# Cross keys computed at the exit of a convolution, gate transposes moved behind two expert units, and a sigmoid table requested early

## What is computed

```python
x = x + L0_attn(layernorm(x))     # causal self-attention, 16 heads
x = x + L0_conv(layernorm(x))     # long convolution with a gate: y = irfft(rfft(kv)*rfft(k)) + kv*skip; out = y . ctx
x = x + L0_ffn(layernorm(x))      # mixture of experts: 2 shared, 16 routed
x = x + L1_attn(layernorm(x))     # causal self-attention
x = x + L1_xattn(layernorm(x), ctx)   # cross attention; its keys and values come from ctx alone
x = x + L1_ffn(layernorm(x))      # 32 experts, 4 per token

# L0_ffn
out = flat + sum_shared(relu(flat @ w1 + b1) @ w2 + b2)
scores = sigmoid(flat @ centroids.T) + bias
vals, idx = top_k(scores, 4)
gating = scatter(vals, idx); gating = gating / sum(gating)
out = out + sum_e gating[:, e] * (relu(flat @ w1[e] + b1[e]) @ w2[e] + b2[e])
```

## Time and profile before

| | us |
|---|---|
| median of three runs | 576.19 (575.97 to 577.64) |
| the profiled execution's own time | 570.98 |
| its span | 569.2 |
| from the end of the convolution's last product to the end of the router scores | 141.2 to 160.5 |
| from there to the first `down` | 160.5 to 168.9 |
| the expert loop on PE | 168.9 to 286.9 |

### The profile page before, as it was taken

How to read it: one execution, slowest core, us unless ns; L and a number is a source line. 1 busy time by engine, 2 the same in 40 slices (tenths; PEclk the granted TensorE clock), 3 DMA queues, 4 the chain that set the end, 5 groups by cost and what they waited for, 6 DMA issues and landing times.

```text
span 569.2 us, 13098 instructions
## 1 busy us (share of the span) xinstructions
PE 535.0 (94%) x4933; PEld 341.4 (60%) x4933; DVE 360.8 (63%) x795; ACT 259.6 (46%) x533; POOL 319.5 (56%) x395
## 2 busy tenths in 40 slices
PE   7999998999999999999998999987999998899998
PEld 4556765444656666665665566664555554466687
DVE  5456864999865555543487567776687757972341
ACT  2315553000395666563454355645566567104530
POOL 3448754989675444331044699859799973540000
PEclk9999999999999999999999999999999999999999
DMA  8996028000006333331303994011120022028311
GB/s 279 109 133 282 3 102 372 0 0 1 0 7 223 111 95 108 96 108 55 99 27 47 124 196 167 1 30 29 43 91 2 2 70 99 1 86 303 122 45 59
DMA packets 25134, 53.05 MB, mean 93 GB/s; under 512 B 3515, under 2 KB 16333, under 8 KB 23153
## 3 DMA queue, kind: packets, MB, share of 16 engines
q1 hardware_dynamic: 24357, 51.01, 32.7%
q10 hardware_dynamic: 716, 1.21, 0.6%
HBM read 41.51 MB, written 1.12 MB: 75 GB/s over the span
## 4 chain that ended last, share of the span: by engine, by line
PE 62%; DVE 17%; POOL 8%; ACT 5%; issue 4%; SPq 2%; DMA 1%; ACTq 0%; POOLq 0%; DVEq 0%
PE PS L1394 57%; POOL R L614 6%; PE PS L1398 4%; DVE R L1240 4%; DVE R L1237 3%; DVE mx L1141 2%; DVE R L424 2%; DVE xn L1029 1%; SPq L445 1%; PE PS L1417 1%; ACT xnT L754 1%; POOL rstd L563 1%; PE PS L1853 1%; DVE X L1019 1%; DVE stats L1014 1%
## 5 line engine op out<-in xcount | busy, mean ns | idle before, releaser
L1394 PE MATMUL PS<-R 128*128 128x256 f16 (+5 forms) x1864 | 184.6, 273 | 2.7 <-DVE R L1296 1.4
L1394 PEld LDWEIGHTS PS<-R 128*128 128x128 f16 (+4 forms) x1864 | 123.1, 102 | 70.6 <-issue 42.2
L1141 DVE TENSOR_REDUCE mx<-PS 128x4 bf16<-128x512 f32 x128 | 82.4, 686 | 36.5 <-PE PS L1394 27.3
L840 ACT ACTIVATE R<-PS 128x512 f32<-128x512 f32 x128 | 69.4, 594 | 65.3 <-PE PS L1394 65.1
L1394 PE MATMUL PS<-xnT,R 128*128 128x512 f16 (+1 forms) x348 | 83.3, 379 | 1.4 <-ACT xnT L754 1.4
L614 POOL TENSOR_TENSOR R<-mx,causal 128x512 bf16<-128x512 bf16 x64 | 65.5, 1044 | 31.7 <-DVE mx L1141 30.3
L1287 DVE TENSOR_TENSOR R<-R,wr 128x512 f32<-128x512 f32 (+1 forms) x46 | 33.3, 723 | 57.3 <-ACT R L939 53.6
L614 POOL TENSOR_TENSOR R<-mx,R 128x512 bf16<-128x512 bf16 x64 | 65.3, 1043 | 6.3 <-DVE mx L1141 6.2
L939 ACT ACTIVATE R<-PS,small 128x512 f32<-128x512 f32 (+1 forms) x50 | 34.3, 686 | 48.9 <-PE PS L1394 48.9
L1394 PEld LDWEIGHTS PS<-xnT,R 128*128 128x128 f16 (+1 forms) x348 | 33.8, 99 | 33.6 <-ACT xnT L754 2.0
L1394 PE MATMUL PS<-negidb,R 128*128 128x128 bf16 x512 | 41.9, 219 | 3.8 <-ACT R L840 2.0
(11 more groups left out here) (206 smaller groups left out, 819.2 us busy)
## 6 DMA issues: line engine op xcount, KB each, us to landing
R<-in_experts_dram SPq DMA_DIRECT2D x5, 1536.0 KB, 8.3
R<-R SPq DMA_DIRECT2D x48, 128.0 KB, 7.0
wr<-g_scr SPq DMA_DIRECT2D x16, 256.0 KB, 3.2
R<-in_w_dram SPq DMA_DIRECT2D x1, 3200.0 KB, 17.5
R<-in_w_dram SPq DMA_DIRECT2D x1, 3168.0 KB, 10.3
WT<-in_wt_a_dram SPq DMA_DIRECT2D x2, 1024.0 KB, 11.7
R<-in_toe_dram SPq DMA_DIRECT2D x1, 2048.0 KB, 13.9
wr<-g_scr SPq DMA_DIRECT2D x10, 192.0 KB, 2.8
```

The source lines that it names most:

```text
L840: s.activation(PTm[:, n % 4, 4 * k:4 * k + 4, :], bank(2 + (2 * n + k) % 3).rearrange("p (h q) -> p h q", h=4), ACT.Exp, scale=c["sc"]).th ...
L1141: v.tensor_reduce(mx[:, n % 4, 4 * k:4 * k + 4], bank(k).rearrange("p (h k) -> p h k", h=4), AX.X, ALU.max).then_inc(S("att_mx"), 1)
L1394: return nc.tensor.matmul(o_, l, r, start=start, stop=stop)
```

## The change

Three edits, all in the order of instructions; no arithmetic is added or removed, apart from fillers and one one-element activation.

1. **Cross keys earlier.** `cross_keys` takes the half as argument and uses banks 1 and 2. On PE the first half takes the place of the ten fillers behind the last skip product, and the second half the place of the ten fillers ahead of the turned sequences. ACT makes the bias of the first half behind `block_high(0..1)`, with waits for the last use of the context in `CT`, and of the second half behind the fourth copy of turned sequences. DVE makes the low part of the first half after the eighth `conv_update`, and of the second half, with the values' bias (`cross_rows`), after the last `normalise`. Fillers beside them use other banks, and `up(1)` and the router scores wait until the banks of the keys have been read.
2. **Gate transposes later.** They stand behind `down(0)`, `up(4)` and `down(1)`, in banks 2 and 3; PE waits for the copied gates only ahead of `down(4)`. ACT's `gates()` moves from unit 3 to unit 4.
3. **Sigmoid table early.** ACT runs a sigmoid on one element (`warm`) behind the first half of the keys.

```diff
@@ ACT
+            act.wait_ge(S("ub"), B)
+            act.wait_ge(S("wb_ready"), B)
+            cross_keys(0)
+            s.activation(warm[:, :], ident[:, 0:1], ACT.Sigmoid)
             for half in range(NH):
 ...
                 if half == 0:
+                    cross_keys(1)
                     weights_high("w16r", cen16[:, 0], cenT)
 ...
             for i in range(N0):
-                if i == 2:
-                    cross_keys()
-                if i == 3:
+                if i == 4:
                     gates()
@@ DVE
             for b in range(6, B):
                 conv_update(b)
+            cross_keys(0)
             for b in range(4, B):
                 normalise(2, b)
+            cross_keys(1)
+            cross_rows()
 ...
-                if i == 2:
-                    cross_keys()
@@ PE
-            def cross_keys():
-                pe.wait_ge(S("x_updated"), 2 * B)
-                for half in range(NH):
-                    for dc in range(DC):
-                        ins = mm(bank(6 + half, parts=64), wkv[:, 0, dc, :], ctxT[:, dc, half * HF:(half + 1) * HF], dc == 0, dc == 1)
-                    ins.then_inc(S("kx_ps"), 1)
+            def cross_keys(half):
+
+                pe.wait_ge(S("z"), DC * CH - 2 + half)
+                for dc in range(DC):
+                    ins = mm(bank(1 + half, parts=64), wkv[:, 0, dc, :], ctxT[:, dc, half * HF:(half + 1) * HF], dc == 0, dc == 1)
+                ins.then_inc(S("kx_ps"), 1)
 ...
-            keep_busy(10, 7)
+            cross_keys(0)
             pe.wait_ge(S("oT"), DC * CH)
 ...
-            keep_busy(10, 2)
+            cross_keys(1)
             for b in range(4):
                 xnt(2, b)
-                keep_busy(2, 2)
-            keep_busy(4, 2)
+                keep_busy(2, 0)
+            keep_busy(4, 0)
             pe.wait_ge(S("xnT_ready"), 2 * B + 4)
             up(0)
+            pe.wait_ge(S("kx_lo"), 1)
             up(1)
 ...
+            pe.wait_ge(S("kx_lo"), NH)
             pe.wait_ge(S("xnT_ready"), 3 * B)
 ...
-            cross_keys()
             up(2)
             up(3)
-            pe.wait_ge(S("gf0"), 1)
-            for b in range(B):
-                ins = tr(PS[0:NE0, 4 + b // 4, b % 4 * P:(b % 4 + 1) * P], gf0[:, b, :])
-                if b % 4 == 3:
-                    ins.then_inc(S("g0T_ps"), 1)
-            pe.wait_ge(S("g0T"), NH)
+
+            def gates_by_expert():
+                pe.wait_ge(S("gf0"), 1)
+                for b in range(B):
+                    ins = tr(PS[0:NE0, 2 + b // 4, b % 4 * P:(b % 4 + 1) * P], gf0[:, b, :])
+                    if b % 4 == 3:
+                        ins.then_inc(S("g0T_ps"), 1)
+
 ...
             for i in range(N0):
                 if 1 <= i < N0 - 3:
                     up(i + 3)
-                if i == 2:
-                    pe.wait_ge(S("kx_lo"), NH)
+                if i == 4:
+                    pe.wait_ge(S("g0T"), NH)
                 down(i)
+                if i == 1:
+                    gates_by_expert()
```

28 lines of the change are left out of this document (14 added, 14 removed).

## The result

Beside each other on one chip, in 20 runs each, the changed kernel has a median of 579.47 us (577.18 to 584.99) and the kernel before 576.02 (573.06 to 582.18). The ratio is 1.0068, with a 95% interval of 1.0044 to 1.0093. The time lies 1.1 above the forecast of 578.4 and inside the range.

The account below looks back on a forecast made before the run. PE, busy 94% of the span, was taken as the bound, without slack behind the first `down`. `down(3)` at 178.9 instead of 176.71 gave +2.2: 576.19 + 2.2 = 578.4 us, range 576.6 to 581.2.

Parts of the forecast that it names:

- The rival of the clock: PE's new idle stretches lower its clock to 1.2 GHz; one slow pair gives +4.8 us, 581.0; chance 0.12.
- list of signs: Wrong if PE has no gap ahead of down(3), first down is after 168, or clock below full at 161 to 190.
- Exit of the convolution: Four key instructions replace ten fillers, so the transposes start 0.3 us later, with ends 0.2 and 0.4.
- The second half of the keys: Ahead of the turned sequences: the first comes 0.24 us late, the next catch up; counted as nothing, at worst 0.2.
- Sigmoid: Without the table load beside the scores, the sigmoid follows them at about 160.8, 0.15 us earlier than before.
- Start of the experts: down(0) no longer waits behind gate transposes and ACT's copies; it starts at 167.27, 1.6 us earlier.
- `up(2)` and `up(3)` ... end well ahead; their time isn't on the path: Ahead of down(0), these products needn't wait for the keys and so add nothing to the time.
- The way round of the gates: From transposes through DRAM to first gated product: 6.4 us, upper end 7.04; that product starts at 177.6, 4.0 later.
- The order on DVE: Unit 3's low part stands behind unit 4's gated product, ends 1.3 us after its start, and delays down(3).
- The sum: down(3) starts at 178.9 instead of 176.71, +2.2 us, with ends +0.9 and +2.85.
- The slack ahead of `down(7)`: Of 2.5 us slack behind the fifth gated product 1.8 is used, 0.7 left; it holds, narrowly.
- The gaps forecast: PE idles 2.7 us behind the scores, 1.0 between up(3) and down(0), and 2.8 ahead of down(3).

Follow-up runs that it names:

- e3_fillers: The changed kernel with 24 filler matmuls between the scores and up(2); 582.49 us, ratio 1.0113 to the kernel before.
- e6_turn_first_fill: The changed kernel with gate transposes ahead of down(0), their wait still ahead of down(4), and 24 fillers ahead of up(2); 573.27 us, ratio 0.9950 to before.
- e10_turn_behind_first: The changed kernel with 24 fillers ahead of up(2) and gate transposes behind down(0) instead of down(1); 576.46 us, ratio 1.0005 to before.
- e9_both_filled: The changed kernel with 24 fillers ahead of up(2) and 26 ahead of down(3); 579.05 us, ratio 1.0071 to the kernel before.

## Why the prediction was right

The sign, the mechanism and the place were right: the gates come about as late as forecast, DVE meets them ahead of the low part of unit 3, and `down(3)` waits. The rival of the clock came true beside the forecast, not in its stead. By the prediction's own list of signs, two of the three that would show it wrong stand in the profile after: the first `down` at 28.25, which is 168.9 in the frame of before and later than 168, and a granted clock of 0.50 between 168 and 175 us. The third, a PE without a gap ahead of `down(3)`, doesn't. Point by point:

- **Exit of the convolution.** Mis-sized. +0.3 was forecast, with 0.4 as the upper end, and +0.50 measured (2.39 against 1.89). The transposes started 1.86 after the keys' start, so they waited for nearly all of the four passes (1.93); hardly any tail was saved. By the scores it had grown to +0.59. The second half of the keys, counted at nothing with 0.2 at worst, is left with the remaining 0.1: the first turned sequence came 0.87 late (10.96 against 10.09), and most of that was caught up as forecast.
- **Sigmoid.** It came 0.11 later, not 0.15 earlier, all of it from the term above: the scores are 0.59 late, and without a load the sigmoid follows them at once (0.87 idle, released by PE). The table alone gives the 0.47 that the step had in mind. The trace with the keys alone shows once more an activation that starts as its table load ends (163.00 + 1.28, then 164.29), as the earlier trace rows did, and no drain behind it, against the Trainium skill's figure (page "ScalarE: Activation LUTs", section "What ACT_TABLE_LOAD costs").
- **Start of the experts.** At full clock `down(0)` starts at 26.94, where the forecast had 26.6: the 0.3 of the two points above. In the profiled execution of the changed kernel it starts at 28.25, not earlier than before at all. The step "`up(2)` and `up(3)` ... end well ahead; their time isn't on the path" failed: at 1.2 GHz they end at 28.5 and are the path.
- **The way round of the gates.** 6.4 was forecast and 7.04 the upper end; it measured 6.4 with the gates alone, 6.55 with both gaps filled and 6.7 in the changed kernel, but 7.1 with the low part of unit 3 first and 8.6 with half of the keys early, so 7.04 is no bound for other orders. ACT did stand waiting (3.26) and copied as the transposes went.
- **The order on DVE.** As forecast: `down(3)` behind the first gated product by 1.35 (1.3 forecast), and taking the low part out of that place removes the wait.
- **The sum.** +2.2 forecast; 2.43 with the gates alone, 2.70 with all edits at full clock. The difference of 0.5 is 0.3 of the exit of the convolution, 0.15 of the way round and the rounding of the low part.
- **The slack ahead of `down(7)`.** "It holds, narrowly" failed in the profiled execution. 0.7 was left, and the fifth gated product waited 3.93 for its rows, so that PE stood 1.28. The load had taken 10.67, where the kernel before had 8.5 at most and the other traces 6.3 to 10.0. (The prediction calls the low part behind the fifth gated product, unit 8's, that of its own unit; it is unit 7's, the one that `down(7)` needs, so the sum stands.) With both gaps filled it held (`down(10)` keeps the 2.70 of `down(3)`), and so it did with the first gap filled and with the gates alone moved, where what `down(10)` lost behind `down(3)`, 1.7, is the clock's. It is a cost of some executions, and how often it falls due was not measured.
- **The clock.** The gaps forecast were 2.7, 1.0 and 2.8, and the first and third are there (2.78 and 3.13). The middle one isn't there in the changed kernel, since the slow products fill it; with these at full speed it was 1.03 (transposes one pair earlier). That the clock would fall had got a chance of 0.12, since no row could tell; it fell in the profiles of all seven kernels that left such a gap unfilled (2.77 to 3.21 us), behind one of the gaps or, with the low part of unit 3 first, behind both. This rival was given too little. The price of a pair, 2.6, was about right (the two `up` products 2.54 more, `down(3)` and one `up` 1.7), but the first fall is half hidden (1.3 at `down(0)`), and the rival's +4.8 was not reached in the median.

So the stall, which the prediction had named and sized at 2.2, is 2.4 to 2.7 in the traces, and is the larger part of the median's +3.45. The rest, about 1, is put down to the clock by subtraction. How large the clock's part is stays open: the line through the runs gives it 2.4 of 4.0, but the kernel with both gaps filled, which has the same stall and no more time at the lower level than before (6.7 against 6.8 us), was 3.16 slower in the median, which would leave 0.3. That the median came to within 1.1 of the forecast is in part luck, since a fall of the clock as large as one pair (+2.6) was not in the sum and came only in part. What decides, in one execution, behind which gap the clock falls is open too: in the changed kernel's profile the second gap, 3.13 long, was followed by a `down(3)` at full speed (1.48), in three others 2.82, 2.93 and 2.98 were not.

## What to carry to other kernels

Ask of an instruction that is moved later not only who needs its result, but what stands in the queue of the engine that waits for it: here `down(3)` needed nothing of the gates and still paid for them, since an in-order engine had their product ahead of an ungated low part. Leave the start of a long round trip (transpose, copy, store, load) as early as it can stand and move only the wait for it; with that the change went from 0.7% slower to no measurable difference (0.9982), and with fillers in the gap that was left to 0.5% faster (0.9950), though these two can't be told apart by their times. When work is taken out of a place where PE would otherwise be idle, look for the new gaps and for slow products behind them in the trace. Fillers restore the clock behind the gap in which they stand, but they don't pay for a stall: with both gaps filled the changed kernel was no faster than without (1.0071 against 1.0068), and with one filled it was no better either (1.0113).

## What the hardware showed that was not expected

The clock also fell where the profile shows no idle time of PE just before. In the trace with the gates alone moved, in the expert loop, products with only 18 rows of 128 (`b2cat`) were followed by slow ones. Timeline:

```profile
271.69 0.69 PE L1394 MATMUL PS<-b2cat,R 18*128 18x256 f32 x2
272.32 2.61 PE L1394 MATMUL PS<-xnT,R 128*128 128x512 f16 x6
274.72 2.06 PE L1394 MATMUL PS<-R 128*128 128x256 f16 x12
```

and the window on it:

```profile
272.00:274.00 2.00, 2.00 (x7) 0.70 (x6) 0.00 (x0) 0.00 (x0) 0.00 (x0) 0.62 0.01 2
```

PE is busy for 2.00 of 2.00 us, at a granted clock of 0.62. The same place is slow in the profiles of three more kernels (`e3_fillers`, `e6_turn_first_fill`, `e10_turn_behind_first`), an `up` a little earlier behind the same kind of product in `e9_both_filled` and again in `e10_turn_behind_first`, and all are at full speed in the other eight profiles, that of the kernel before among them. All four kernels with 24 fillers are in the first group and only one of the other nine. With one profile of each, neither this nor the few rows is shown to be the cause; nobody should count the fillers as free before that is tried. It may be one of the sources of the 6.8 us at the lower level that even the kernel before has on the mean of its runs, while its profiled execution, with full clock in every slice, took less (570.98) than any of the 20 runs beside the changed kernel (573.06 at least); whoever reads that page alone doesn't see that the typical run of this kernel has some time at the lower clock.
